# Local attention and feed-forward on one core: GpSimd adds the second bias and finishes the tile, VectorE adds the variance's addend, and two steps change places in VectorE's and ScalarE's orders

## The reference

```python
h = _layernorm(x, axis=-1) * (1 + cb) + sb
x = x + gb * ffn(h)
...
def _layer(x, ...):                       # two layers
    h = shift_token(x)                    # half of the features come from the token before
    q, k, v = split(h @ wqkv)             # 8 heads of 64
    q = l2norm(q) * qs; k = l2norm(k) * ksc
    q, k = rotary_xpos(q, k)
    o = local_attention(q, k, v)          # windows of 128 tokens, each also sees the one before
    x = x + o @ wo
    h = shift_token(x)
    h = (h - mean(h)) / sqrt(var(h) + 1e-05) * lg + lb
    a, g = split(h @ w1 + b1)             # 2 x 682
    x = x + (a * gelu(g)) @ w2 + b2
    return x
```

## Time and profile before

| | |
|---|---|
| median of 3 runs | 5170.97 us (5169.97 to 5171.83) |
| the profiled execution | 5168.58 us, its span 5166.8 us |
| TensorE busy | 4816.6 us (93%) |
| VectorE busy | 3875.0 us (75%) |
| ScalarE busy | 2870.5 us (56%) |
| GpSimd busy | 1175.7 us (23%) |
| mean granted clock of TensorE | 0.986 of 2.4 GHz |

### The profile page before, as it was taken

How to read it: one execution, slowest core, us unless ns; L and a number is a source line. 1 busy time by engine, 2 the same in 40 slices (tenths; PEclk the granted TensorE clock), 3 DMA queues, 4 the chain that set the end, 5 groups by cost and what they waited for, 6 DMA issues and landing times.

```text
span 5166.8 us, 85245 instructions
## 1 busy us (share of the span) xinstructions
PE 4816.6 (93%) x29996; PEld 2901.3 (56%) x29996; DVE 3875.0 (75%) x10911; ACT 2870.5 (56%) x6033; POOL 1175.7 (23%) x1722
## 2 busy tenths in 40 slices
PE   3899999999999997999999999999999999999998
PEld 1233333333333324777777777777777777777776
DVE  3788888787888874777777777777777777777776
ACT  1466656666666663555555555555555555555554
POOL 2112021111202002222322222222222222222222
PEclk7899999999999998999999999999999999999999
DMA  4333233322423221000000000000000000000000
GB/s 117 91 56 71 49 66 46 70 53 50 68 58 66 31 38 38 7 7 5 7 6 29 7 6 6 7 6 28 5 7 7 5 7 25 10 7 6 6 5 5
DMA packets 156572, 153.87 MB, mean 30 GB/s; under 512 B 25236, under 2 KB 148584, under 8 KB 156016
## 3 DMA queue, kind: packets, MB, share of 16 engines
q1 hardware_dynamic: 156144, 148.42, 14.0%
HBM read 103.49 MB, written 44.09 MB: 29 GB/s over the span
## 4 chain that ended last, share of the span: by engine, by line
PE 74%; DVE 13%; issue 4%; ACT 3%; SPq 3%; DMA 2%; POOL 2%; DVEq 0%; POOLq 0%; ACTq 0%
PE psum L864 13%; PE psum L628 8%; PE psum L646 7%; PE psum L782 7%; PE psum L658 6%; PE psum L874 5%; PE psum L830 5%; PE psum L791 4%; PE psum L821 4%; PE psum L813 4%; DVE mx L1128 3%; DVE big_s L1329 3%; PE psum L839 2%; PE psum L611 2%; PE psum L803 1%
## 5 line engine op out<-in xcount | busy, mean ns | idle before, releaser
L1128 DVE TENSOR_REDUCE mx<-psum 128x1 f32<-128x512 f32 x2048 | 1334.5, 685 | 310.7 <-PE psum L628 305.9
L935 ACT ACTIVATE pr<-psum 128x1024 f32<-128x1024 f32 x1024 | 1021.2, 1023 | 634.2 <-PE psum L646 622.8
L628 PE MATMUL psum<-stack 96*128 96x512 bf16 x2048 | 727.4, 389 | 61.2 <-DMA stack<-parts_d 19.1
L864 PE MATMUL psum<-hlT_s,w_sb 128*114 128x128 f32 (+1 forms) x6144 | 740.6, 274 | 30.0 <-ACT hlT_s L1012 30.0
L864 PEld LDWEIGHTS psum<-hlT_s,w_sb 128*114 128x114 f32 (+1 forms) x6144 | 702.0, 178 | 76.6 <-ACT hlT_s L1012 60.5
L998 ACT ACTIVATE big_s<-big_s,mxl_s 128x256 f32<-128x256 f32 x1024 | 508.7, 499 | 302.1 <-DVE mxl_s L1334 302.1
L646 PE MATMUL psum<-stack 99*128 99x512 bf16 x2048 | 613.6, 381 | 15.3 <-DMA stack<-mrow 14.7
L628 PEld LDWEIGHTS psum<-stack 96*128 96x128 bf16 x2048 | 196.5, 96 | 747.9 <-DVE mx L1128 284.7
L1526 POOL TENSOR_TENSOR rn_s<-ss_s,neghalf 128x4 f32<-128x4 f32 x512 | 549.9, 1074 | 75.9
L658 PE MATMUL psum<-pr,vg 128*32 128x512 f32 x4096 | 547.1, 606 | 0.4 <-ACT pr L935 0.4
L782 PE MATMUL psum<-wqkv_sb,uT_s 128*128 128x512 f32 x1024 | 506.7, 607 | 0.7 <-DVE uT_s L1286 0.7
(11 more groups left out here) (159 smaller groups left out, 6728.4 us busy)
## 6 DMA issues: line engine op xcount, KB each, us to landing
stack<-parts_d SPq DMA_DIRECT2D x384, 128.0 KB, 5.8
parts_d<-parts SPq DMA_DIRECT2D x64, 384.0 KB, 2.8
hn<-in_x SPq DMA_DIRECT2D x8, 1024.0 KB, 9.2
xr<-in_x SPq DMA_DIRECT2D x8, 1024.0 KB, 5.3
x_d<-xr SPq DMA_DIRECT2D x8, 1024.0 KB, 9.4
tab<-tab_d SPq DMA_DIRECT2D x32, 256.0 KB, 2.6
out_x<-o_s SPq DMA_DIRECT2D x64, 128.0 KB, 1.7
xs<-x_d SPq DMA_DIRECT2D x8, 896.0 KB, 7.6
```

Of the source, the lines that this page charges most:

```text
L628: pe.matmul(psum[:, to, :], stack[0:KS, g % 2, 0, u % 2, h, a * P:(a + 1) * P], stack[0:KS, g % 2, 1, kh, h, :], start=True, stop=True).th ...
L864: mm = pe.matmul(psum[0:rows, bk + G_BANK[j], m * P:(m + 1) * P], w1_sb[:, l, k, col:col + rows], w["hlT"][:, k, :], start=(k == 0), stop= ...
L935: act.activation(pr[:, e % 2, 2 * pair:2 * pair + 2, :], psum[:, 2 * pair:2 * pair + 2, :], ACT.Exp, scale=DH ** -0.5).then_inc(s_exp, 1)
L1128: dve.tensor_reduce(mx[:, u % 2, m, kh:kh + 1], psum[:, src, :], AX.X, ALU.max).then_inc(s_max, 1)
```

## The change

Three steps change their engine, and two places change in the orders of VectorE and ScalarE.

- ub, the sum of u1 and the second bias, and fin, the two sums of a finished tile, go from VectorE to GpSimd. GpSimd does ub of X, fin of Y and fin of X behind rqb of Y at the start of a round, and ub of Y behind ln of Y. In layer 0 ub waits for the fin ahead of it, since it writes the tile that fin reads.
- The addend of the variance (rs) goes from GpSimd to VectorE, into the step ag. GpSimd keeps the power alone.
- In VectorE's order knb of X stands ahead of m0 of X and no longer behind u1 of Y.
- In ScalarE's order qcb and kcb of Y stand ahead of e0 of Y.

```diff
@@ scalar
-            rounds(("ge0X:1 ge1X:1 qcaY:1 kcaY:1 ge2X:1 e0Y:1 qcbY:1 kcbY:1 e1Y:1 sqaX:0 e2Y:1 e3Y:1 pc0Y:1 pc1Y:1 sqbX:0 pc2Y:1 "
+            rounds(("ge0X:1 ge1X:1 qcaY:1 kcaY:1 ge2X:1 qcbY:1 kcbY:1 e0Y:1 e1Y:1 sqaX:0 e2Y:1 e3Y:1 pc0Y:1 pc1Y:1 sqbX:0 pc2Y:1 "
@@ vector
-                elif name == "fin":
-                    if l == 1:
...
-                        dve.tensor_tensor(w["o"][:], w["u"][:], gateF[:, s], ALU.mult).then_inc(w["s_oo"], 1)
-                        dve.wait_ge(w["s_oo"], it * 2 + 1)
-                        dve.tensor_tensor(w["o"][:], w["o"][:], x1, ALU.add).then_inc(w["s_oo"], 1)
...
                     dve.bn_aggr(w["mv"][:], w["st"][:].rearrange("p a n -> p (a n)")).then_inc(w["s_ln_ag"], 1)
+                    dve.wait_ge(w["s_ln_ag"], n * 4 + 3)
+                    dve.tensor_scalar(w["rs"][:], w["mv"][:, 1:2], LN_EPS, None, ALU.add).then_inc(w["s_ln_ag"], 1)
                 elif name == "hl":
-                    dve.wait_ge(w["s_ln_rs"], n * 2 + 2)
+                    dve.wait_ge(w["s_ln_rs"], n + 1)
...
-                elif name == "ub":
-                    dve.wait_ge(w["s_u1"], n + 1)
-                    dve.tensor_tensor(w["u"][:], w["u1"][:, l, own, :], b2_sb[:, l], ALU.add).then_inc(w["s_u2"], 1)
...
-            rounds(("rsbY:1 rotbY:1 adbY:1 ac0X:1 knbY:1 ac1X:1 ac2X:1 finY:2 m0Y:1 ubX:1 u2X:1 d0Y:1 uTcX:0 d1Y:1 m1Y:1 rsaX:0 "
-                    "ssaX:0 d2Y:1 rotaX:0 d3Y:1 adaX:0 knaX:0 rotbX:0 ssbX:0 rsbX:0 adbX:0 m0X:0 u1Y:1 knbX:0 bnuY:1 bnsY:1 agY:1 "
-                    "d0X:0 hlY:1 m1X:0 d1X:0 d2X:0 finX:1 d3X:0 lnY:0 ubY:1 ac0Y:1 ac1Y:1 leY:0 ac2Y:1 u2Y:1 uTcY:0 u1X:0 bnuX:0 "
+            rounds(("rsbY:1 rotbY:1 adbY:1 ac0X:1 knbY:1 ac1X:1 ac2X:1 m0Y:1 u2X:1 d0Y:1 uTcX:0 d1Y:1 m1Y:1 rsaX:0 "
+                    "ssaX:0 d2Y:1 rotaX:0 d3Y:1 adaX:0 knaX:0 rotbX:0 ssbX:0 rsbX:0 adbX:0 knbX:0 m0X:0 u1Y:1 bnuY:1 bnsY:1 agY:1 "
+                    "d0X:0 hlY:1 m1X:0 d1X:0 d2X:0 d3X:0 lnY:0 ac0Y:1 ac1Y:1 leY:0 ac2Y:1 u2Y:1 uTcY:0 u1X:0 bnuX:0 "
                     "lnX:-1 bnsX:0 agX:0 hlX:0 ssaY:0 rsaY:0 rotaY:0 adaY:0 knaY:0 leX:-1 ssbY:0"), step_dve)
@@ gpsimd
                 elif name == "rs":
-                    gp.wait_ge(w["s_ln_ag"], n * 3 + 3)
-                    gp.nop(nofuse=True)
-                    gp.tensor_scalar(w["rs"][:], w["mv"][:, 1:2], LN_EPS, 1.0, ALU.add, ALU.mult).then_inc(w["s_ln_rs"], 1)
-                    gp.wait_ge(w["s_ln_rs"], n * 2 + 1)
+                    gp.wait_ge(w["s_ln_ag"], n * 4 + 4)
                     gp.nop(nofuse=True)
                     gp.tensor_tensor(w["rs"][:], w["rs"][:], neghalf[:, 0:1], ALU.pow).then_inc(w["s_ln_rs"], 1)
+                elif name == "ub":
+                    gp.wait_ge(w["s_u1"], n + 1)
+                    if l == 0 and it > 0:
+                        gp.wait_ge(w["s_oo"], it * 2)
+                    gp.nop(nofuse=True)
+                    gp.tensor_tensor(w["u"][:], w["u1"][:, l, t % 2, :], b2_sb[:, l], ALU.add).then_inc(w["s_u2"], 1)
+                elif name == "fin":
+                    if l == 1:
...
+                        gp.tensor_tensor(w["o"][:], w["u"][:], gateF[:, w["bk"] // 4], ALU.mult).then_inc(w["s_oo"], 1)
+                        gp.wait_ge(w["s_oo"], it * 2 + 1)
+                        gp.nop(nofuse=True)
+                        gp.tensor_tensor(w["o"][:], w["o"][:], xs[:, w["bk"] // 4, t, :], ALU.add).then_inc(w["s_oo"], 1)
...
-            rounds(("rqbY:1 rkaX:0 rqaX:0 rkbX:0 rqbX:0 rsY:1 lnY:0 lnX:-1 rsX:0 rkaY:0 rqaY:0 rkbY:0"), step_pool)
+            rounds(("rqbY:1 ubX:1 finY:2 finX:1 rkaX:0 rqaX:0 rkbX:0 rqbX:0 rsY:1 lnY:0 ubY:1 lnX:-1 rsX:0 rkaY:0 rqaY:0 rkbY:0"), step_pool)
```

More of the change, by code:

```diff
@@ L1354, in step_dve @@
                 elif name == "ag":
-                    dve.wait_ge(w["s_ln_ag"], n * 3 + 2)
+                    dve.wait_ge(w["s_ln_ag"], n * 4 + 2)
                     dve.nop(nofuse=True)
                     dve.bn_aggr(w["mv"][:], w["st"][:].rearrange("p a n -> p (a n)")).then_inc(w["s_ln_ag"], 1)
+                    dve.wait_ge(w["s_ln_ag"], n * 4 + 3)
+                    dve.tensor_scalar(w["rs"][:], w["mv"][:, 1:2], LN_EPS, None, ALU.add).then_inc(w["s_ln_ag"], 1)
                 elif name == "hl":
-                    dve.wait_ge(w["s_ln_rs"], n * 2 + 2)
+                    dve.wait_ge(w["s_ln_rs"], n + 1)
                     for k, src in ((0, w["u1"][:, l, own, 0:P]), (1, psum[:, bk, 0:P])):
@@ L1527, in step_pool @@
                 elif name == "rs":
-                    gp.wait_ge(w["s_ln_ag"], n * 3 + 3)
-                    gp.nop(nofuse=True)
-                    gp.tensor_scalar(w["rs"][:], w["mv"][:, 1:2], LN_EPS, 1.0, ALU.add, ALU.mult).then_inc(w["s_ln_rs"], 1)
-                    gp.wait_ge(w["s_ln_rs"], n * 2 + 1)
+                    gp.wait_ge(w["s_ln_ag"], n * 4 + 4)
                     gp.nop(nofuse=True)
                     gp.tensor_tensor(w["rs"][:], w["rs"][:], neghalf[:, 0:1], ALU.pow).then_inc(w["s_ln_rs"], 1)
+                elif name == "ub":
[6 more added lines that the diff above has]
+                    if l == 1:
+                        if t == 0:
+                            gp.wait_ge(s_xs_in, 64 * i + 64)
+                        gp.wait_ge(w["s_u2"], n * 2 + 2)
+                        gp.wait_ge(w["s_out"], FREE + it * 16)
+                        gp.nop(nofuse=True)
+                        gp.tensor_tensor(w["o"][:], w["u"][:], gateF[:, w["bk"] // 4], ALU.mult).then_inc(w["s_oo"], 1)
+                        gp.wait_ge(w["s_oo"], it * 2 + 1)
+                        gp.nop(nofuse=True)
+                        gp.tensor_tensor(w["o"][:], w["o"][:], xs[:, w["bk"] // 4, t, :], ALU.add).then_inc(w["s_oo"], 1)
                 else:
```

## The result

The change makes the kernel slower: 5290.7 us (median of four runs, 5284.0 to 5295.5) beside 5170.9 us (four runs, 5170.0 to 5171.8), a ratio of 1.0227 with a 95% interval of 1.0212 to 1.0243. The prediction had the direction and the main mechanism, but 5290.7 lies outside its range of 5225 to 5275; it is 44 us over the forecast. Of all executions behind the numbers from here on one was slow, 8961 us at a mean granted clock of 0.78 for the version with ScalarE's order alone, and is left out of its median.

The account below looks back on a forecast made before the run. TensorE was taken to bound the kernel, working 2744 of 2900 us, so added stalls count in full. 91.5 - 10.6 - 8.3 + 3 = +76 us gave 5247 us beside 5171, range 5225 to 5275.

Parts of the forecast that it names:

- e0: ScalarE's first exponential of Y: forecast to start at 3111.60 instead of 3110.11 in an odd round, behind copies and table load.
- Part 1: ScalarE: qcb and kcb of Y ahead of e0 delay the exponential's table load; 1.26 us lost per odd round, 1.65 per even, 91.5 together.
- Part 2: Variance's addend from GpSimd to VectorE: power starts earlier; -10.6 us for X in odd rounds, -8.3 us for Y.
- part 3: ub and fin moved from VectorE to GpSimd: cost nothing, except the last fin, under 1 us.
- rival B: GpSimd's longer sums hold up VectorE at hl or d0 of Y: 5267 us for one, 5290 for both; chance 0.08.
- The sum without the clock: Sum of the parts, no clock fall: 91.5 - 10.6 - 8.3 + 3 = +76 us, giving 5247 us.
- Part 4: VectorE: knb of X ahead of m0 fits in 1.0 us of idle time; effect zero.
- rival C: TensorE's clock falls behind the new gap: 13 us if one round of ten, 120 if all; chance 0.04 of over 30 us.

## Why the prediction was right and wrong

**Part 1 was right, in mechanism and size.** The load moved with the first exponential, the delay ran over d0 and uT's copy, and the new wait is 1.65 us in odd and 1.58 in even rounds. Alone it costs 2.90 us per pair of rounds at the full clock, forecast 2.91.

**Part 2 was mis-sized, to the safe side.** Alone it wins 26 us, forecast 19. The larger miss is Y's, 64 x 0.07 = 4.5 us: the start of the power was well placed (0.25 us earlier forecast, 0.28 measured), but it takes only 0.08 us longer beside d0's products (0.63, not 0.55) and not the 0.12 that was set against it. X's is 32 x 0.08 = 2.6 us: 0.33 was taken, and TensorE lost all of its wait of 0.41. In the changed kernel part of the gain is taken back again, by the next point.

**"Cost nothing" for part 3 was wrong.** It was rival B in small. In one odd round of the changed kernel:

```profile
2965.91 0.73 POOL L1526 TENSOR_TENSOR u_s<-u_s,b_sb 128x256 f32<-128x256 f32 x1
2966.06 0.65 DVE L1354 TENSOR_SCALAR hl_s<-u_s,mv_s,rs_s 128x128 f32<-128x128 f32 x1
...
2967.09 0.44 PE L854 MATMUL psum<-ident,hl_s 128*128 128x128 f32 x2 [0.58 <-DVE hl_s L1354]
```

hl waits behind ub, and TensorE waits 0.58 us where an even round has 0.27: 32 x 0.3, some 10 us. The other place named, d0 of Y beside fin of X in even rounds, is missed, as the changed kernel's timeline shows:

```profile
2999.46 0.73 POOL L1537 TENSOR_TENSOR o_s<-o_s,xs 128x256 f32<-128x256 f32 x1
...
3000.43 0.62 DVE L1333 TENSOR_SCALAR big_s<-big_s,rz_s 128x256 f32<-128x256 f32 x2
```

The second sum ends at 3000.19, and d0's two products run from 3000.43 on undisturbed. As forecast the table load keeps them apart: with ScalarE's order put back they meet, and TensorE waits 7.3 us for uT. The forecast priced a hit at up to 0.7 us, and hl's is 0.3 since part of the sum is over when hl comes. The Trainium skill, "SBUF — State Buffer", section "Who interferes with whom", says that when VectorE works in a mode that takes both port pairs, which a tensor_scalar like hl can enter, whoever issues first holds the pair that it shares with GpSimd and the other blocks fully. The trace agrees as far as it shows: hl issues second and ends within 0.1 us of ub's end.

**The sum without the clock was right, in part by luck.** 5247.2 us were measured with the gap filled, forecast 5247. But two errors cancel: part 2 won 7 us more than its term, and hl's meeting with ub cost 10 where the sum had nothing. Pairs of rounds at the full clock went from 98.74 to 101.05 us (50.76 + 50.29), 2.31 more; the forecast's terms give 2.91 - 0.33 - 0.26 = 2.32. Part 4 was not tried alone, so its share is not known. Parts 2 and 3 apart give -26 + 10 = -16 us, and with part 4 the three give -20, a difference no larger than the spread of such runs.

**The step that failed is the one that gave rival C 0.04 and the range room for one round in ten.** The mechanism was named: a gap of 1.6 us behind 1.1 us of work and a shorter gap, and up to 2 us each time. The price held (1.6 us), but it fell on 26 rounds of 63, which is 42 us by TensorE's busy time and 43.5 us by the filled gap. The reason given for the small chance, that the place had never shown it before, was no evidence. Before the change the gap was not there, and the forecast itself said that it would be. The only row shown on what idle time does to the clock was the earlier trace rows, with far more of it, and it spoke for a fall. The forecast also took the falls for rare exceptions, where the runs show that the gap meets the beat of the clock in 15 to 26 rounds of 63.

## What to carry to other kernels

When a stall lands on TensorE, price it twice: its own length, and what TensorE's next products cost at half the clock. If the trace has never shown a gap of that length, the case with falls belongs into the range and perhaps into the forecast, and as a share of the rounds, since not every gap met one here; where the gap can't be removed, cheap products put into it can be worth more than nothing (43 us here). And look in ScalarE's compiled order for where the table loads go when activations change places: a load goes with the first activation of its kind, and one cheap activation placed early can put it back into idle time. Moving sums from VectorE to GpSimd is free only where no short VectorE step on the critical path runs beside them.

## What the runs showed of the hardware

- A wait of 1.57 to 1.65 us, with one of 0.52 us shortly ahead of it, was enough to bring the granted clock to 0.50 in some rounds: the groups behind it took 3.38 to 3.78 us instead of 1.98, in 26 rounds of 63 in one kernel and in 15 of 63 in another with the same wait. Slow were exactly the rounds in which one of the evenly spaced instants at which the clock can change came between 0.60 us before and 0.31 us after the end of the wait. With 1.53 us of it filled by 12 small turns, the clock didn't fall once in the stage, in two executions.
- Waits of 0.75 and 0.92 us with 1.13 us of work between them were enough for one fall, in a version that had no longer gap.
- GpSimd's sum of two operands over 256 columns of float32 takes 0.73 us, close to the 0.7 that was estimated from the row of 512. GpSimd's instructions by line and form in the changed kernel, 2100 to 5100 us:

```profile
L1526 POOL TENSOR_TENSOR u_s<-u_s,b_sb 128x256 f32<-128x256 f32 x118 | 85.8, 727 | 0.0
```

- VectorE steps that come behind the start of such a sum end 0.02 to 0.09 us behind its end: hl grows from 0.35 to 0.65 or 0.73 us, and a step of four columns from 0.17 to 0.51. The two products of d0, which GpSimd's two sums run beside, grow from 0.62 to 1.18.
